# Keys turned later in the step: a move on TensorE and ScalarE in an attention kernel with a routed feed-forward

## The chip, the cores and the metric

The kernel runs on one core of one Trainium2 chip. The metric is the device time of one execution in microseconds (us). The engines are TensorE (PE; its weight loads are listed apart as PEld), VectorE (DVE), ScalarE (ACT), GpSimd (POOL) and SyncE (SP). Matmul results land in PSUM, eight banks of 128 partitions by 512 fp32 words.

## The reference

A block with a residual: layernorm of x (8 batches of 1024 rows, 128 wide), a causal attention that is linear in its scores, and a feed-forward with eight experts of which each row uses two.

```python
q, k, v = heads(Wq), heads(Wk), heads(Wv)            # 16 heads of 64
q = q / max_norm(q); k = k / max_norm(k)             # per batch and head
num = cumsum(v) + einsum(q, cumsum(k outer v))
den = arange(1, n + 1) + einsum(q, cumsum(k))
attn = (num / den) @ Wo.T + bo
probs = softmax(xn @ router_w); top 2, renormalised
expert_out = (silu(xn @ gate[e]) * (xn @ up[e])) @ down[e]
out = x + attn + sum over the two experts of weight * expert_out
```

## The kernel before

The program has an attention phase (up to about 950 us of the profile), a phase that runs tiles of 128 sorted rows through the experts, and a phase that adds the parts. Only the attention phase is touched.

Rows are handled in 64 chunks of 128 (8 batches of 8 chunks). The main loop has a step for each chunk g; c = g % 8 is its place in the batch and b its batch. Each step does several things for different chunks, so that the engines have something to do while they wait for each other. In order, PE issues in a step: `heads_from(g)` (for two groups hg of four head pairs the products with the running sums, L1273 and L1281, then the causal part within the chunk, L1292), `values(g + 2)` (L1157 to L1159 with 512 columns), `project(g - 1)` (output projection, L1329), `outer(g + 1)` (outer products of keys and values, L1307), `keys(g + 2)` (the keys turned, L1241), `scores(g + 2)` (L1255; with c = 0 also `scores(g + 1)`; none with c = 6 and 7), `rank` (with c = 3), `norms` (L1194), `fill` (keys or queries of the next batch, L1157 to L1159 with 256 columns), with an even c also `logits` (8 columns), and `turn(g)` (the finished heads turned, L1318). A step with c = 7 has an order of its own, since the next batch's scale is worked out there, and it is not changed. In the last batch there are no `norms`, `fill` and `logits`.

The small matmuls use part of the array. The profile prints rows*columns of the part: `outer`, `scores` and all of `heads_from` are 64*64, `keys` and `turn` are 64*128, `norms` is 128*32, the rest 128*128.

DVE takes in a step: `heads` (division and copy out, L847 to L856), `x_lo` (with c = 0, 2, 4, 5), `attended` (L880), `state` (adds the outer products to the running sums, L876), `mask` (scores times the causal mask, L839), small routing work (`choose_first`, `choose_second`, `place_rows`) or statistics, `norm_max` (L795), four copies out of `fill` (L785), and with an even c the copy of the logits (L791). With c = 3 `place_rows` lies between `mask` and the copies, with c = 6 `values_parts` (L808 to L815) and `batch_scale`. ACT takes `heads_out(g - 1)` (L591), `values_out` (L585), `keys_out(g + 2)` (L580), `scale_q` (L598), sometimes `normalise` (L561), and four `square` (L574).

PSUM banks are given out by a rule: `psum_order` lists the jobs in the order in which PE does them, job n takes bank n % 8, and before its first matmul PE waits (`wait_bank`) until the job eight places earlier has been read out. The table `FREED` says which semaphore tells that: `e_f` counts the copies of `fill`, `e_L` those of the logits, `e_A` masks, `e_kn` the two halves of `keys_out`, `e_st` states, `e_mx` norm_max, `e_num` heads, `e_nT` heads_out. So the order of the jobs also decides what a matmul waits for. `heads_from` needs four banks, two for each hg; `wait_bank` for the second two is asked just before the second group.

Of the kernel before, what the change touches and what calls it, by code (L numbers as in the profile page):

```python
# [10 lines left out]
C = B * N // P  # L11
# [23 lines left out]
def build(nc, x, wkq, wv, wo, bo, rw, gate_up_w, down_head, down_tail, out):  # L35
# [9 lines left out]
    with ctx:  # L45
# [216 lines left out]
        def psum_order():  # L262
# [22 lines left out]
            for g in range(C):  # L285
                b, c = g // CB, g % CB
                G, more = NCP * (b + 1) + c // 2, b < B - 1
                if c == 0 and g > 0:
                    yield ("O", g - 1)
                yield from uses_N(g)  # L290
                if c == CB - 1 and more:
                    yield from uses_norm(G, 0)
                    yield from uses_fills(G, 1)
                    yield from uses_V(g + 2)
                    yield from uses_norm(G, 1)
                    yield ("O", g - 1)
                    yield from uses_T(g)
                    yield ("C", b + 1)
                    yield from uses_D(g + 1)
                    yield from uses_KT(g + 2)  # L300
                    yield from uses_S(g + 1)
                    continue
                if c in (0, 2, 4) and more:
                    yield from uses_x(G)
                if g + 2 < C:
                    yield from uses_V(g + 2)
                if c == 5 and more:
                    yield from uses_x(G + 1)
                if c == 6 and more:
                    yield ("VC", b + 1)  # L310
                if c > 0:
                    yield ("O", g - 1)
                if g + 1 < C:
                    yield from uses_D(g + 1)
                if g + 2 < C:
                    yield from uses_KT(g + 2)
                if c == 0:
                    yield from uses_S(g + 1)
                if c < CB - 2:
                    yield from uses_S(g + 2)  # L320
                if c == rank_at(b):
                    yield ("R", b)
                if more:
                    if c > 0:
                        yield from uses_norm(G - 1 + c % 2, 1 - c % 2)
                    yield from uses_fills(G, c % 2)
                    if c % 2 == 0:
                        yield from uses_logits(G)
                yield from uses_T(g)
            yield ("O", C - 1)  # L330

# [216 lines left out]
        def _(act):  # L548
# [97 lines left out]
            for g in range(C):  # L646
# [24 lines left out]
                if c == rank_at(b):  # L671
                    act.wait_ge(s_mm, b + 1)
                    act.activation(mm[:], mm[:], ACT.Exp).then_inc(s_exp, 1)
                if g + 2 < C:
                    keys_out(g + 2)
                if c + 3 < CB:
                    scale_q(b, c + 3)
                if c == 5 and b < B - 2:
# [7 lines left out]
                if more:  # L686
                    for f in range(4):
                        square(G, 4 * (c % 2) + f)
                if b == B - 1 and c >= 6:
                    if c == 6:  # L690
                        act.wait_ge(f_w, 16)
                        act.wait_ge(a_N, 2 * (g - 1) + 2)
                        act.wait_ge(f_te, 1)
                    for e in range(4 * (c - 6), 4 * (c - 6) + 4):
                        act.activation(guh[:, e], gu[:, e], ACT.Copy).then_inc(f_wh, 1)
# [454 lines left out]
        def _(pe):  # L1150
# [206 lines left out]
            for g in range(C):  # L1357
# [27 lines left out]
                    project(g - 1)  # L1385
                if g + 1 < C:
                    outer(g + 1)
                if g + 2 < C:
                    keys(g + 2)
                if c == 0:  # L1390
                    scores(g + 1)
                if c < CB - 2:
# [3 lines left out]
                if more:  # L1396
# [3 lines left out]
                        fill(G, 4 * (c % 2) + f)  # L1400
                    if c % 2 == 0:
                        logits(G)
                turn(g)
            project(C - 1)
            pe.wait_ge(e_y, C)
# [97 lines left out]
```

## Time and profile before

| | us |
|---|---|
| median of 3 runs | 1316.72 |
| lowest and highest run | 1312.32 to 1317.18 |
| the profiled execution's own time | 1315.11 |
| its span in the trace | 1313.3 |
| PE busy | 1194.2 (91%) |
| DVE busy | 940.2 (72%) |
| ACT busy | 707.7 (54%) |

The span is what the trace covers; the execution's own time is 1.8 us more. A busy PE is the time in which a matmul was in flight, and two that overlap are counted once, so a run of small matmuls looks as dense as a run of large ones. In the timeline each row is a merged run of instructions of one line: its start, its length up to the end of the last, the line, the operation, the names, the part of the array, the shape and the count. The length overlaps the next row by the time that the last matmul takes to end; what a run costs the engine is read from its start to the start of the row behind it. A bracket gives idle time before the row and what ended it; "issue" is time in which the engine waited for nothing that the profile shows.

### The profile page before, as it was taken

To read this page: it belongs to the slowest core of one execution; us is meant where nothing else is said; L and a number is where in the kernel's file an instruction comes from. 1 tells how busy PE (TensorE), PEld (TensorE's weight loads), DVE (VectorE), ACT (ScalarE), POOL (GpSimd) and SP (SyncE) were. 2 spreads that over 40 slices of the span, in tenths; PEclk is the share of its full clock that TensorE was granted. 3 is DMA by queue.
4 is the path that set the end of the run, shared out by engine and by line. 5 is a ranking of instruction groups with operands and counts; after the bars stand their busy time and mean duration, and the time that the engine had idled before them with its cause. 6 is when DMAs were issued, how large, how long until landed. Compare 5 with 4: busy or idle time off the path is not lost.

```text
span 1313.3 us, 60282 instructions
## 1 busy us (share of the span) xinstructions
PE 1194.2 (91%) x24400; PEld 1053.6 (80%) x24401; DVE 940.2 (72%) x2662; ACT 707.7 (54%) x1683; POOL 366.5 (28%) x599
## 2 busy tenths in 40 slices
PE   6789999999999999999899999998869999999950
PEld 5478878878887887888788788877869999999950
DVE  6778778877877877787788778778845555555534
ACT  4466566647656664665666466555524444444420
POOL 5100111111211111121112111112735555555546
PEclk9999999999999999999999999999979999999985
DMA  6000000000000000000000000020122222222228
GB/s 216 3 4 6 11 12 12 16 11 12 16 12 11 12 17 11 12 14 14 11 12 14 13 12 14 14 99 19 43 84 62 61 61 63 63 61 61 63 84 332
DMA packets 36136, 54.66 MB, mean 42 GB/s; under 512 B 7504, under 2 KB 26608, under 8 KB 35664
## 3 DMA queue, kind: packets, MB, share of 16 engines
q1 hardware_dynamic: 25744, 29.02, 7.2%
q0 software_dynamic: 9024, 18.20, 4.1%
q8 instruction: 179, 2.93, 1.0%
q10 hardware_dynamic: 1152, 4.19, 0.8%
q14 instruction: 37, 0.30, 0.1%
HBM read 28.33 MB, written 23.06 MB: 39 GB/s over the span
## 4 chain that ended last, share of the span: by engine, by line
PE 77%; DVE 14%; issue 4%; DMA 2%; ACT 1%; POOL 1%; SPq 0%; POOLq 0%; DVEq 0%; ACTq 0%
PE bank L1157 10%; PE bank L1159 9%; PE bank L1158 9%; PE bank L1329 8%; PE bank L1436 7%; PE bank L1307 5%; PE bank L1255 5%; PE bank L1292 4%; PE bank L1281 4%; PE bank L1194 4%; PE bank L1429 3%; PE bank L1241 3%; DVE qs L785 2%; PE bank L1318 2%; PE bank L1273 2%
## 5 line engine op out<-in xcount | busy, mean ns | idle before, releaser
L478 POOL COPY xn<-meta 128x2 f32<-128x2 f32 x128 | 26.4, 206 | 712.3 <-PE bank L1292 711.0
L535 POOL DMA_INDIRECT expert_rows<-yt,wdi x136 | 132.6, 975 | 142.4 <-ACT yt L707 116.0
L1157 PE MATMUL bank<-xTh,Wh 128*128 128x256 f32 x512 | 153.0, 299 | 5.0 <-DVEq L812 2.5
L580 ACT ACTIVATE kn<-bank 128x512 f32<-128x512 f32 x128 | 69.5, 595 | 151.9 <-PE bank L1241 151.9
L598 ACT ACTIVATE qs<-qs,cvec 128x128 f32<-128x128 f32 x480 | 146.0, 394 | 0.2 <-DVE cvec L831 0.2
L1158 PE MATMUL bank<-xTh,Wl 128*128 128x256 f32 x512 | 146.0, 285 | 0.0
L1159 PE MATMUL bank<-xTl,Wh 128*128 128x256 f32 x512 | 145.8, 285 | 0.0
L1157 PEld LDWEIGHTS bank<-xTh,Wh 128*128 128x128 f32 x512 | 98.9, 193 | 53.1 <-issue 46.6
L1329 PEld LDWEIGHTS bank<-WoT,numT 128*128 128x128 f32 x1024 | 123.4, 194 | 17.4 <-issue 12.6
L482 POOL DMA_INDIRECT sorted_tokens<-xn,slot x128 | 125.7, 982 | 39.1 <-POOL xn L478 39.1
L1113 DVE TENSOR_TENSOR xtTl<-bank,xtTh 128x128 fp32r<-128x128 f32 x137 | 40.0, 292 | 128.9 <-ACT xtTh L702 119.8
L1329 PE MATMUL bank<-WoT,numT 128*128 128x128 f32 x1024 | 129.1, 280 | 2.1 <-ACT numT L591 1.3
L1436 PE MATMUL bank<-dn,aT 128*128 x828 | 119.5, 281 | 0.0
L707 ACT ACTIVATE yt<-bank,wd 128x128 f32<-128x128 f32 x138 | 50.7, 368 | 122.7 <-PE bank L1436 122.7
L1157 PE MATMUL bank<-guh,xtTh 128*128 x272 | 111.7, 410 | 3.2 <-DVE xtTl L1113 1.6
L856 DVE TENSOR_TENSOR num<-bank,rden 64x256 f32<-64x256 f32 x256 | 108.0, 422 | 8.0
L574 ACT ACTIVATE sq<-ks 128x512 f32<-128x512 f32 x128 | 77.3, 630 | 64.6 <-DVE ks L785 57.6
L839 DVE SCALAR_TENSOR_TENSOR A<-bank,causal 128x512 f32<-128x512 f32 x128 | 82.0, 686 | 41.0 <-PE bank L1255 41.0
L585 ACT ACTIVATE vaug<-bank 128x512 f32<-128x512 f32 x128 | 75.4, 597 | 66.0 <-PE bank L1159 61.4
L1436 PEld LDWEIGHTS bank<-dn,aT 128*128 128x128 f32 x828 | 105.1, 192 | 6.9 <-issue 0.4
L574 ACT ACTIVATE sq<-qs 128x512 f32<-128x512 f32 x128 | 77.5, 630 | 53.1 <-DVE qs L785 44.8
L1158 PEld LDWEIGHTS bank<-xTh,Wl 128*128 128x128 f32 x512 | 99.1, 194 | 0.2 <-issue 0.2
(211 smaller groups left out, 2947.6 us busy)
## 6 DMA issues: line engine op xcount, KB each, us to landing
xt<-sorted_tokens SPq DMA_DIRECT2D x137, 66.0 KB
er<-expert_rows SPq DMA_DIRECT2D x16, 512.0 KB, 6.8
xa<-in_x SPq DMA_DIRECT2D x8, 512.0 KB, 11.2
out<-ot ACTq DMA_DIRECT2D x8, 512.0 KB, 6.9
gu<-in_gate_up_w SPq DMA_DIRECT2D x1, 2816.0 KB, 10.3
expert_rows<-yt,wdi POOLq DMA_INDIRECT x136
sorted_tokens<-xn,slot POOLq DMA_INDIRECT x128, 2.3
wraw<-in_wkq SPq DMA_DIRECT2D x2, 512.0 KB, 5.7
```

The costliest lines, as they stand in the source:

```text
L482: pool.indirect_dma_start(xs_d, bass.IndirectOffsetOnAxis(ap=slot[:, g % XR, k:k + 1], axis=0), xn[:, g % XR, :], None).then_inc(c_out[k][ ...
L535: pool.indirect_dma_start(ys_d, bass.IndirectOffsetOnAxis(ap=wdi[:, r:r + 1], axis=0), yt[:, r, :], None).then_inc(f_sc[r], 16)
L574: act.activation(sq[:, f % 4], src[:, G % NCP, 2 * (f % 4):2 * (f % 4) + 2, :].rearrange("p h i -> p (h i)"), ACT.Square).then_inc(e_sq, 1)
L585: act.activation(vaug[:, g % 2, par, :, 0:DH], pbank("V", g, par)[:].rearrange("p (h e) -> p h e", e=DH), ACT.Copy).then_inc(e_v, 1)
L598: last = act.activation(q_, q_, ACT.Copy, scale=cvec[:, p:p + 1])
L839: dve.scalar_tensor_tensor(A[:, g % 2, par], pbank("S", g, par)[:].rearrange("p (h i) -> p h i", i=DH), 1.0, causal[:].unsqueeze(1).broadc ...
L856: last = dve.tensor_tensor(num[halves(t), 4 * hg:4 * hg + 4, 1, :], v[halves(1 - t), :, 0:DH], rden[halves(1 - t), hg, 1].unsqueeze(2).bro ...
L1157: pe.matmul(dst, ah, bh, start=start, stop=False)
L1158: pe.matmul(dst, al, bh, start=False, stop=False)
L1159: return pe.matmul(dst, ah, bl, start=False, stop=stop)
L1329: last = pe.matmul(pbank("O", g)[:, 0:D], numT[:, p, :], WoT[:, p, :], start=(p == 0), stop=(p == HP - 1))
L1436: last = pe.matmul(bank[6 + s][:, 0:D], aT[:, s, t, :], dn[:, t, bass.ds(ex, 1), :].rearrange("p a f -> p (a f)"), start=(t == 0), stop=(t ...
```

## The change

`keys(g + 2)` moves from behind `outer(g + 1)` to a place directly ahead of `turn(g)`, in every step that has it except c = 7, and `keys_out(g + 2)` on ACT moves from behind `values_out` to a place behind the squares. `psum_order` follows, and so do the banks. No instruction is added or removed, and the order on DVE, POOL and SP is as before.

```diff
@@ psum_order
                 if g + 1 < C:
                     yield from uses_D(g + 1)
-                if g + 2 < C:
-                    yield from uses_KT(g + 2)
                 if c == 0:
                     yield from uses_S(g + 1)
...
                     if c % 2 == 0:
                         yield from uses_logits(G)
+                if g + 2 < C:
+                    yield from uses_KT(g + 2)
                 yield from uses_T(g)
@@ block.scalar
-                if g + 2 < C:
-                    keys_out(g + 2)
                 if c + 3 < CB:
                     scale_q(b, c + 3)
...
                     for f in range(4):
                         square(G, 4 * (c % 2) + f)
+                if g + 2 < C:
+                    keys_out(g + 2)
@@ block.tensor
                 if g + 1 < C:
                     outer(g + 1)
-                if g + 2 < C:
-                    keys(g + 2)
                 if c == 0:
                     scores(g + 1)
...
                     if c % 2 == 0:
                         logits(G)
+                if g + 2 < C:
+                    keys(g + 2)
                 turn(g)
```

On PE, in the middle of a step (here c = 2 of the first batch), from the projection to the first fill, before:

```order
L1329 MATMUL bank<-WoT,numT 128x128 x8
L1307 MATMUL bank<-vaug,kn 64x65 x32
L1241 MATMUL bank<-ident,ks 128x64 x16
L1255 MATMUL bank<-qs,ks 64x64 x32
L1227 MATMUL bank<-rowsum,before 128x8
L1228 MATMUL bank<-rowsum,ones 128x8
```

and after the change:

```order
L1329 MATMUL bank<-WoT,numT 128x128 x8
L1307 MATMUL bank<-vaug,kn 64x65 x32
L1255 MATMUL bank<-qs,ks 64x64 x32
L1227 MATMUL bank<-rowsum,before 128x8
L1228 MATMUL bank<-rowsum,ones 128x8
```

The turned keys (L1241) have left the place between the outer products (L1307) and the scores (L1255).

On PE, at the end of a step with c = 6 (the first batch), from the end of the logits to the second group of the next `heads_from`, with the semaphores that a row waits for, before:

```order
L1159 MATMUL bank<-rwl,xTh 128x8
L1318 MATMUL bank<-ident,num 128x64 [waits e_num,e_n1,e_kn]
L1318 MATMUL bank<-ident,num 128x64 x15
L1273 MATMUL bank<-VC,sel 64x260 [waits e_vc,e_st,e_f,e_mx]
L1273 MATMUL bank<-VC,sel 64x260 x3
L1281 MATMUL bank<-st,qs 64x65 x16
L1273 MATMUL bank<-VC,sel 64x260 [waits e_st,e_f]
L1273 MATMUL bank<-VC,sel 64x260 x3
L1281 MATMUL bank<-st,qs 64x65 x16
```

and after the change:

```order
L1159 MATMUL bank<-rwl,xTh 128x8
L1241 MATMUL bank<-ident,ks 128x64 [waits e_f,e_st]
L1241 MATMUL bank<-ident,ks 128x64 x15
L1318 MATMUL bank<-ident,num 128x64 [waits e_num,e_n1,e_f,e_mx]
L1318 MATMUL bank<-ident,num 128x64 x15
L1273 MATMUL bank<-VC,sel 64x260 [waits e_vc,e_st,e_f]
L1273 MATMUL bank<-VC,sel 64x260 x3
L1281 MATMUL bank<-st,qs 64x65 x16
L1273 MATMUL bank<-VC,sel 64x260 [waits e_st,e_L,e_f]
L1273 MATMUL bank<-VC,sel 64x260 x3
L1281 MATMUL bank<-st,qs 64x65 x16
```

The turned keys stand ahead of `turn` (L1318). The turned heads now wait for a fill's copy and `norm_max` (`e_f`, `e_mx`) instead of `keys_out` (`e_kn`), and the second group (the second L1273) waits for the copy of the logits (`e_L`) as well, which is the last of DVE's copies in the step.

On ACT, from `values_out` of the step with c = 1 of the first batch to that of the next step, before:

```order
L585 ACTIVATE vaug<-bank 128x8x64 x2
L580 ACTIVATE kn<-bank 128x512 x2
L598 ACTIVATE qs<-qs,cvec 128x128 x8
L561 ACTIVATE xn<-xa,nmr,rstd 128x128 x2
L574 ACTIVATE sq<-qs 128x512 x4
L591 ACTIVATE numT<-bank 128x8x64 x2
L566 ACTIVATE xTh<-bank 128x256
L585 ACTIVATE vaug<-bank 128x8x64 x2
```

and after the change:

```order
L585 ACTIVATE vaug<-bank 128x8x64 x2
L598 ACTIVATE qs<-qs,cvec 128x128 x8
L561 ACTIVATE xn<-xa,nmr,rstd 128x128 x2
L574 ACTIVATE sq<-qs 128x512 x4
L580 ACTIVATE kn<-bank 128x512 x2
L591 ACTIVATE numT<-bank 128x8x64 x2
L566 ACTIVATE xTh<-bank 128x256
L585 ACTIVATE vaug<-bank 128x8x64 x2
```

`keys_out` (L580) stands behind the squares (L574) and directly ahead of `heads_out` (L591).

How the places eight earlier in the order of the jobs change, for the waits that the prediction speaks of (hg 0 and hg 1 are the two groups of `heads_from`; fills of a step are numbered 1 to 4):

| wait at the end of step | before | after |
|---|---|---|
| c = 1, 3, 5: hg 0 | no fill, at the latest norms | fills 1 and 2 |
| c = 1, 3, 5: hg 1 | fills 1 and 2 | fills 3 and 4 |
| c = 0, 2, 4: hg 0 | norms or scores, and fill 1 | fills 2 and 3 |
| c = 0, 2, 4: hg 1 | fills 2 and 3 | fill 4 and the logits |
| c = 6: hg 0 | norms and fill 1 | fills 2 and 3 |
| c = 6: hg 1 | fills 2 and 3 | fill 4 and the logits |
| last batch, c = 0: hg 0 | both halves of `keys_out` | the two masks of the first scores |
| last batch, c = 0: hg 1 | the two masks of the first scores | the two masks of the second scores |

## Rows read from the trace of the kernel before

**Rows 1.** Busy time, 120 to 840 us: PE, PEld, DVE, ACT, POOL, clock.
```profile
120.00:840.00 720.00, 694.77 (x17368) 597.94 (x17368) 568.60 (x1593) 439.53 (x984) 114.37 (x198) 1.00 0.04 13
```

**Rows 2.** Waits of PE between 120 and 850 us: total us, times, longest.
```profile
PE bank L1255 <- issue: 4.9, 5, 1.5
...
PE bank L1273 <- DVE ks L785: 2.9, 8, 0.4
PE bank L1273 <- DVE qs L785: 2.3, 6, 0.4
```

**Rows 3.** PE, a step with c = 1: start us, length us, line.
```profile
435.48 1.17 PE L1307 MATMUL bank<-vaug,kn 64*64 64x65 f32 x64
436.57 0.71 PE L1241 MATMUL bank<-ident,ks 64*128 64x64 f32 x16
437.21 1.16 PE L1255 MATMUL bank<-qs,ks 64*64 64x64 f32 x64
438.31 1.07 PE L1194 MATMUL bank<-sq,nsel 128*32 128x512 f32 x8
...
442.36 0.71 PE L1318 MATMUL bank<-ident,num 64*128 64x64 f32 x16
443.00 0.30 PE L1273 MATMUL bank<-VC,sel 64*64 64x260 bf16 x4
443.14 0.64 PE L1281 MATMUL bank<-st,qs 64*64 64x65 f32 x32
443.61 0.28 PE L1273 MATMUL bank<-VC,sel 64*64 64x260 bf16 x4
```

**Rows 4.** Timeline of PE in a step with c = 0.
```profile
307.99 2.10 PE L1255 MATMUL bank<-qs,ks 64*64 64x64 f32 x128
310.01 0.39 PE L1157 MATMUL bank<-xTh,Wh 128*128 128x256 f32 x1
```

**Rows 5.** Timeline of DVE in the step of rows 3.
```profile
440.63 2.53 DVE L785 COPY qs<-bank 128x512 f32<-128x512 f32 x4
```

**Rows 6.** Timeline of DVE in a step with c = 3.
```profile
464.24 1.57 DVE L876 TENSOR_TENSOR st<-bank,st 128x260 f32<-128x260 f32 x4 [0.36 <-PE bank L1307]
466.44 1.29 DVE L839 SCALAR_TENSOR_TENSOR A<-bank,causal 128x512 f32<-128x512 f32 x2 [0.63 <-PE bank L1255]
...
470.94 2.48 DVE L785 COPY qs<-bank 128x512 f32<-128x512 f32 x4
```

**Rows 7.** Timeline of PE where that step ends.
```profile
472.32 0.30 PE L1273 MATMUL bank<-VC,sel 64*64 64x260 bf16 x4 [0.40 <-DVE qs L785]
```

**Rows 8.** Timeline of DVE in a step with c = 6.
```profile
512.24 2.48 DVE L785 COPY ks<-bank 128x512 f32<-128x512 f32 x4
514.62 0.17 DVE L791 COPY L<-bank 128x16 f32<-128x16 f32 x1
```

**Rows 9.** Timeline of PE where that step ends.
```profile
514.21 0.30 PE L1273 MATMUL bank<-VC,sel 64*64 64x260 bf16 x4 [0.42 <-DVE ks L785]
```

**Rows 10.** Timeline of DVE in the step of rows 4.
```profile
309.22 2.48 DVE L839 SCALAR_TENSOR_TENSOR A<-bank,causal 128x512 f32<-128x512 f32 x4 [0.63 <-PE bank L1255]
...
315.65 0.16 DVE L791 COPY L<-bank 128x16 f32<-128x16 f32 x1
```

**Rows 11.** Timeline of PE where that step ends.
```profile
315.24 0.31 PE L1273 MATMUL bank<-VC,sel 64*64 64x260 bf16 x4 [0.17 <-DVE ks L785]
```

**Rows 12.** Timeline of DVE in the last batch, step with c = 0.
```profile
890.04 2.49 DVE L839 SCALAR_TENSOR_TENSOR A<-bank,causal 128x512 f32<-128x512 f32 x4
```

**Rows 13.** Timeline of PE where that step ends.
```profile
891.43 0.30 PE L1273 MATMUL bank<-VC,sel 64*64 64x260 bf16 x4 [1.77 <-DVE A L839]
```

**Rows 14.** Timeline of ACT in the step of rows 3.
```profile
441.41 2.42 ACT L574 ACTIVATE sq<-qs 128x512 f32<-128x512 f32 x4
443.73 1.06 ACT L591 ACTIVATE numT<-bank 128x512 f32<-128x512 f32 x2
```

**Rows 15.** Timeline of PE in the step that follows rows 3.
```profile
446.88 1.39 PE L1329 MATMUL bank<-WoT,numT 128*128 128x128 f32 x11
```

## The prediction

> **What bounds the kernel now.** I read first the table of busy time by stretch. Between 120 and 840 us PE is busy for 694.77 of 720 us (96%), DVE for 568.60 (79%), ACT for 439.53 (61%), with the clock at its upper level all along (1.00) [rows 1]. So in the seven batches that look alike PE sets the pace, and its idle time is small. Then I read who ended it: on the second group of `heads_from` (L1273) PE waited 14 times for a copy of DVE (8 and 6 times, 5.2 us in all, never over 0.4 us), and five times in the scores for "issue", up to 1.5 us [rows 2]. That matters here: DVE is not the bottleneck, but at two places of each batch it is already the last to come. The third view is the timeline of PE, which gives the price of a run of small matmuls from start to start; the fourth is DVE's, at the places where it is late.
>
> **What the move saves on PE.** In a step with c = 1 the outer products take 436.57 - 435.48 = 1.09 us, the turned keys 437.21 - 436.57 = 0.64, the scores 438.31 - 437.21 = 1.10, the turned heads 443.00 - 442.36 = 0.64 [rows 3]. Where 128 scores follow one another they take 310.01 - 307.99 = 2.02 us, so that a second 64 on the same part of the array (64*64) costs 0.92 and not 1.10 [rows 4]. The difference of 0.17 to 0.18 is what a run pays for its two ends. Outer products next to scores are such a run of 128: 2.02 us instead of 1.09 + 1.10, a saving of 0.17. The matmuls have the same part of the array, the same count and nearly the same width (65 and 64 columns). That kinds may differ shows in `heads_from`: its 32 matmuls of L1281, with another line on either side but all on 64*64, take 443.61 - 443.14 = 0.47 us [rows 3], against 0.46 for half of the second 64.
>
> No row shows two runs on 64*128 next to one another. The saving of keys next to turned heads lies between nothing and the 0.18 of the other run; it could be below nothing only if the two disturbed each other, for which I see no reason, as they use different banks. I take 0.15. The Trainium skill (TensorEngine Tiling (Array Packing), Key Properties) says that a change of the tiling mode drains the engine and a change of tile within a mode does not; by it this seam is free, as 0.15 says, and no run here shows it yet.
>
> So a step gains 0.17 + 0.15 = 0.32 us if nothing else is late. There are 62 steps that turn keys, 7 of them with c = 7, so 55 are changed: in each of the seven like batches c = 0 to 6, in the last c = 0 to 5. All of it at 0.32 would be 17.6 us. That is not what comes out, because of the banks.
>
> **What the move makes late.** Everything between the outer products and the end of the logits comes 2.83 - 2.02 = 0.81 us earlier on PE, measured from the step's start, and `heads_from` of the next step 0.32 us earlier. DVE can't follow by 0.81: its masks wait for the scores, but stand behind `state`, which ends at 464.24 + 1.57 = 465.81, while the mask began at 466.44 [rows 6]. So DVE's masks and all behind them come 0.63 us earlier. At the same time the second group of `heads_from` no longer waits for the second or third copy, but for the last one (and with an even c for the copy of the logits). Whether this costs depends on c:
>
> c = 1, 2, 4, 5. In the step with c = 1 the fourth copy ends at 440.63 + 2.53 = 443.16 [rows 5]; 0.63 earlier that is 442.53, ahead even of the first group, which would start at 443.00 - 0.32 = 442.68 [rows 3]. With c = 2, 4 and 5 DVE ends its copies as early or earlier against PE. Nothing is late; 28 steps gain 0.32: -9.0 us.
>
> c = 3. `place_rows` pushes the four copies back: they begin at 470.94 and take 2.48, 0.62 each. The second ends at 472.18, and the second group of `heads_from` starts at 472.32, 0.14 later, after a wait of 0.40 [rows 6, 7]. After the change the copies begin at 470.31, the fourth ends at 472.79, and the group starts at 472.93: 0.61 us later than before instead of 0.32 earlier. Seven times: +4.3 us.
>
> c = 6. There are no scores in this step, and `values_parts` and `batch_scale` fix DVE's time from the outer products on, which do not move. The copies of the fills run from 512.24 for 2.48 us, the third ends at 514.10, the group starts at 514.21; the copy of the logits ends at 514.62 + 0.17 = 514.79 [rows 8, 9]. The group now waits for it and starts at 514.91: 0.70 later. Behind it hangs the chain of the batch's end (heads, copies, squares, norms, scale), all of which moves with it. Six times, and 0.4 in batch 6, where `batch_scale` is absent: +4.6 us.
>
> c = 0. Four masks and the bias lie ahead of the copies. The group starts at 315.24 and waited for the third copy; the copy of the logits ends at 315.65 + 0.16 = 315.81 [rows 10, 11]. The masks begin 0.6 earlier, as the scores now take the place of the keys, so it ends at 315.19 and the group starts at 315.30: +0.06, seven times +0.4 us. In the batches in which the scores stall (below) DVE has caught up, and a part of 0.32 may be had.
>
> The last batch. With c = 0 the four masks begin at 890.04 and end 0.62 us apart; the group waits for the second and starts at 891.43 [rows 12, 13]. It now waits for the fourth, which ends at 892.53: +1.25 us, once. The other five changed steps could gain 1.6 us, but each holds a wait for "issue" that ends at its own time; I count half, -0.8.
>
> ACT hides `keys_out` at nothing: the squares end at 441.41 + 2.42 = 443.83, and `heads_out` takes 1.06 [rows 14], `keys_out`, which has the same two copies of 512 columns, about as much. With the squares 0.63 earlier, `keys_out` and `heads_out` behind them end at about 445.3, and `project` needs that at 446.88 - 0.32 = 446.56 [rows 14, 15]: 1.2 us to spare, about half of that with c = 0. If this cover were gone every step would pay. `keys_out` no longer stands ahead of `scale_q`, which can then start while PE still multiplies; that gains nothing, as the scores waited for it only once. Nothing changes in the queues of SP and POOL.
>
> The sum: -9.0 + 4.3 + 4.6 + 0.4 + 1.25 - 0.8 = +0.75 us. The profiled execution took 1315.1 us, 1.8 more than its span, and 1.6 less than the median of the runs, 1316.7. The sum is 1315.9 on the one and 1317.5 on the other. I predict 1316.5.
>
> **Rivals.** *The late copies don't bite* (faster). If the waits at c = 0, 3 and 6 kept their size, all 55 steps would gain 0.32: 17.6 us off the median of 1316.7, 1299. For it: these are 22 of the 55 steps, so an error of mine there weighs much. Against it: the waits exist already, and the table of the banks says that they now name a later copy. Halfway to the forecast it is 1308.
>
> *The saving is not there* (slower). What a run pays at its ends might belong to the change of operands and not of the part of the array. Then the 9.0 and 0.8 fall away and the costs stay: 9.8 above the forecast, 1326. For it: rows 4 join scores to scores, and the outer products have other operands on both sides. Against it: the 32 matmuls of rows 3, whose neighbours are of another kind and which pay nothing at their ends.
>
> *The instructions come too late* (slower). Five times PE waited for "issue" in the scores, up to 1.5 us and 4.9 in all [rows 2]; the long ones were in steps with c = 0, in the middle of a run of 128, the longest dense run of the program. Now every step with c = 1 to 5 has such a run. It decides if a run of 128 is already long enough. At one in five of 35 steps and 1.5 us that is 10.5 above the forecast, 1327. Against it: the two groups of `heads_from` are as dense and as long, and waited so in few steps. The Trainium skill (Runtime: NRT & Kernel Launch, Instruction fetch mechanics) says that instructions are fetched in sequence, in blocks, ahead of their use, and that this is mostly hidden; by it this rival is nothing and the time stays with the sum. The trace does not quite agree: the 1.5 us of rows 2 are not hidden.
>
> **Chances.** The forecast 0.62; late copies don't bite, wholly or in good part, 0.14; the saving is not there 0.07; the instructions 0.12; ACT's spare time used up, or something I do not see, 0.05. What a measurement of this kernel can tell from no change is about 0.5%, 6.6 us, so "no change" is 1310 to 1323. The forecast's own range is 1311 to 1321: the seam of 0 to 0.18 in 28 steps gives +4.2 and -0.8, the runs' own spread some 2.5 to each side. For 8 in 10 I reach to the middle of the rivals: 1305 to 1326. Faster 0.16 (the first rival, and a little of the forecast), no change 0.65, slower 0.19.
>
> **What would show it.** In the profile after, L1307 and L1255 with c = 1 together from start to start 2.0 us (2.2 would say that nothing is saved), L1241 and L1318 together 1.13 (1.28 likewise). PE's waits on L1273 for DVE's copies grow from 5.2 us to about 18, in steps with c = 0, 3 and 6 alone; if they stay at 5 the first rival holds. A step with c = 3 becomes longer by 0.6 us, one with c = 1 shorter by 0.3. If waits for "issue" in L1255 grow to 10 us or more the third rival holds. If `project` waits for `numT`, I have misjudged ACT. The forecast is wrong if the time lies outside 1310 to 1323.

## The result

The changed kernel took 1323.24 us (median of 6 runs, 1319.95 to 1326.72) against 1315.03 of the kernel before (6 runs, 1312.32 to 1317.18): ratio 1.0064, interval 1.0043 to 1.0085, so 8.4 us slower (5.7 to 11.2). The forecast was no change, 1316.5, and wrong by its own words outside 1310 to 1323. The profiled execution took 1320.09 us, with a span of 1318.3.

### The profile page after: what moved, and what is told of

The parts are those of the page before. It is cut to its first block, busy times and chain, and to the rows that moved or that the text cites. A ratio compares the mean times of both kernels' runs of the same rounds, so it can differ in the third digit from the quotient of the medians.

```text
span 1318.3 us, 60282 instructions
## 1 busy us (share of the span) xinstructions
PE 1188.5 (90%) x24400; PEld 1054.3 (80%) x24401; DVE 935.5 (71%) x2662; ACT 703.6 (53%) x1683; POOL 364.6 (28%) x599
## 4 chain that ended last, share of the span: by engine, by line
PE 73%; DVE 18%; issue 5%; DMA 2%; ACT 1%; POOL 1%; SPq 0%; POOLq 0%; DVEq 0%; ACTq 0%
PE bank L1157 9%; PE bank L1158 8%; PE bank L1159 8%; PE bank L1329 8%; PE bank L1436 7%; PE bank L1307 5%; PE bank L1292 5%; PE bank L1281 4%; PE bank L1255 4%; PE bank L1429 3%; PE bank L1194 3%; DVE qs L785 3%; PE bank L1241 2%; PE bank L1273 2%; DVE ks L785 2%
## 5 line engine op out<-in xcount | busy, mean ns | idle before, releaser
L574 ACT ACTIVATE sq<-ks 128x512 f32<-128x512 f32 x128 | 77.2, 630 | 159.7 <-DVE ks L785 152.8
L1329 PEld LDWEIGHTS bank<-WoT,numT 128*128 128x128 f32 x1024 | 123.4, 194 | 17.1 <-issue 12.3
L574 ACT ACTIVATE sq<-qs 128x512 f32<-128x512 f32 x128 | 77.8, 630 | 109.4 <-DVE qs L785 100.1
L847 DVE RECIPROCAL rden<-bank 128x4 f32<-128x4 f32 x256 | 32.2, 167 | 95.2 <-PE bank L1292 93.2
L1159 PEld LDWEIGHTS bank<-xTl,Wh 128*128 128x128 f32 x512 | 99.7, 195 | 0.0
## 6 DMA issues: line engine op xcount, KB each, us to landing
gu<-in_gate_up_w SPq DMA_DIRECT2D x1, 2816.0 KB, 10.5
```

The lines of the kernel that those rows point to most:

```text
L574: act.activation(sq[:, f % 4], src[:, G % NCP, 2 * (f % 4):2 * (f % 4) + 2, :].rearrange("p h i -> p (h i)"), ACT.Square).then_inc(e_sq, 1)
L1159: return pe.matmul(dst, ah, bl, start=False, stop=stop)
L1329: last = pe.matmul(pbank("O", g)[:, 0:D], numT[:, p, :], WoT[:, p, :], start=(p == 0), stop=(p == HP - 1))
```

## The profile after, beside the rows of before

Busy time between 120 and 840 us (columns as in [rows 1]): PE was busy for 694.77 us of this stretch, now for 683.87. The clock is the same, so 11 us more of PE's time are idle, although not one instruction is new.

```profile
120.00:840.00 720.00, 683.87 (x17284) 592.59 (x17276) 562.43 (x1586) 433.96 (x979) 114.12 (x198) 1.00 0.04 13
```

Who ended PE's waits between 120 and 850 us (total, times, longest), to be held against [rows 2]:

```profile
PE bank L1255 <- issue: 7.5, 11, 1.6
PE bank L1273 <- DVE qs L785: 6.1, 14, 0.5
PE bank L1292 <- issue: 5.7, 7, 1.2
PE bank L1318 <- DVE mx L795: 5.0, 6, 0.8
PE bank L1273 <- DVE ks L785: 4.0, 9, 0.5
```

The waits for copies on L1273 grew from 5.2 to 10.1 us, where I had written about 18. A wait of the turned heads for `norm_max` is new (5.0 us, at c = 6) and takes up time that the group behind it would have waited for the copies; together they are 15.1. The line that I had no term for is L1292. The same view of before has these two:

```profile
PE bank L1241 <- issue: 4.0, 6, 0.8
...
PE bank L1292 <- issue: 1.7, 2, 0.9
```

The 4.0 us on L1241 are six waits of the turned keys at c = 0 for a bank (the profile calls them "issue", but each ends just behind `x_lo`, whose semaphore `e_xs` the keys wait for). With the keys gone the scores have them, so L1241 and L1255 together went from 8.9 (11 times) to 7.5 (11 times). On L1292, the second half of `heads_from`, it is 1.7 us, 2 times, before and 5.7 us, 7 times, after.

PE in the step with c = 1, as in [rows 3]:

```profile
438.98 1.16 PE L1307 MATMUL bank<-vaug,kn 64*64 64x65 f32 x64
439.97 1.11 PE L1255 MATMUL bank<-qs,ks 64*64 64x64 f32 x64
441.01 1.07 PE L1194 MATMUL bank<-sq,nsel 128*32 128x512 f32 x8
...
445.06 0.71 PE L1241 MATMUL bank<-ident,ks 64*128 64x64 f32 x16
445.61 0.67 PE L1318 MATMUL bank<-ident,num 64*128 64x64 f32 x16
446.20 0.31 PE L1273 MATMUL bank<-VC,sel 64*64 64x260 bf16 x4
```

From start to start: outer products and scores 441.01 - 438.98 = 2.03 us (2.0 forecast), turned keys and heads 446.20 - 445.06 = 1.14 (1.13 forecast). Before they were 2.19 and 1.28, so the savings are 0.16 and 0.14: 0.30 us per step, where I had 0.32.

DVE at the end of the step with c = 3 (timeline), to be held against [rows 6]:

```profile
474.43 2.47 DVE L785 COPY qs<-bank 128x512 f32<-128x512 f32 x4
```

And PE there, against [rows 7]:

```profile
475.81 0.31 PE L1273 MATMUL bank<-VC,sel 64*64 64x260 bf16 x4 [0.48 <-DVE qs L785]
...
477.01 0.31 PE L1273 MATMUL bank<-VC,sel 64*64 64x260 bf16 x4 [0.43 <-DVE qs L785]
```

The second group now starts behind the fourth copy (474.43 + 2.47 = 476.90, start 477.01), and the first group waits as well, for the second copy. Then the step with c = 6, DVE's last copy against [rows 8]:

```profile
519.45 0.16 DVE L791 COPY L<-bank 128x16 f32<-128x16 f32 x1
```

And PE, against [rows 9]:

```profile
517.84 0.72 PE L1318 MATMUL bank<-ident,num 64*128 64x64 f32 x16 [0.84 <-DVE mx L795]
519.04 0.30 PE L1273 MATMUL bank<-VC,sel 64*64 64x260 bf16 x4 [0.48 <-DVE ks L785]
...
519.72 0.31 PE L1273 MATMUL bank<-VC,sel 64*64 64x260 bf16 x4
```

The second group comes behind the copy of the logits (519.45 + 0.16 = 519.61), as forecast. Both waits ahead of it, for `norm_max` and for the third copy, are new, but they hold up nothing more: the first group starts 1.2 us later against its step, and 0.5 of that comes back, as the second group waits only for its own copy. In one batch they did cost more. There the granted clock fell to 0.50 from 285.9 to 289.2 us, behind the same two waits (0.84 and 0.48 us), and the 64 matmuls of L1292 took 1.96 us instead of 1.13; that step is 1.4 us longer than its like in the other batches. No term of mine has this, and the profile of the kernel before has no such stretch between 80 and 950 us.

The last batch at c = 0, DVE's masks against [rows 12]:

```profile
894.90 2.48 DVE L839 SCALAR_TENSOR_TENSOR A<-bank,causal 128x512 f32<-128x512 f32 x4
```

PE there, against [rows 13]:

```profile
896.29 0.30 PE L1273 MATMUL bank<-VC,sel 64*64 64x260 bf16 x4 [3.04 <-DVE A L839]
896.40 0.76 PE L1281 MATMUL bank<-st,qs 64*64 64x65 f32 x32
897.49 0.43 PE L1273 MATMUL bank<-VC,sel 64*64 64x260 bf16 x4 [0.33 <-DVE A L839]
897.68 1.11 PE L1281 MATMUL bank<-st,qs 64*64 64x65 f32 x32
898.54 1.90 PE L1292 MATMUL bank<-vaug,A 64*64 64x65 f32 x64
900.38 0.50 PE L1157 MATMUL bank<-Wvh,xTh 128*128 128x512 f32 x1
```

The second group stands 2.59 us behind the start of the masks, where it stood 1.39 behind: 1.20 later, 1.25 forecast. But the first group waits too, and PE is idle for 3.04 us in one piece. The table by stretch (columns as before, the granted clock third from the end) shows what follows, here of after:

```profile
896.20:900.00 3.80, 3.38 (x128) 3.25 (x132) 2.53 (x5) 0.00 (x0) 0.18 (x1) 0.58 0.02 4
```

And of before, behind its own wait:

```profile
891.40:895.00 3.60, 3.57 (x110) 3.27 (x111) 3.50 (x8) 0.84 (x2) 1.95 (x3) 1.00 0.02 5
```

The mean granted clock is 0.58 of 2.4 GHz behind the idle time, mostly the lower level of 1.2 GHz, where it was 1.00. From the second group to the values it takes 900.38 - 897.49 = 2.89 us instead of 893.07 - 891.43 = 1.64: 1.25 more, for which I had no term. How much of this the change brings isn't quite sure. With keys late in this step the clock fell here in all four kept profiles (behind waits of 2.3 to 3.0 us); with keys early it fell in five of thirteen (behind 1.7 to 2.0 us), the kernel before not among them.

Part of the delay is given back where the experts begin. PE's first row there, before:

```profile
967.01 0.45 PE L1417 MATMUL bank<-ident,xt 128*128 128x128 f32 x1 [6.45 <-issue]
```

And after:

```profile
973.22 0.45 PE L1417 MATMUL bank<-ident,xt 128*128 128x128 f32 x1 [3.61 <-issue]
```

PE waits there for something that doesn't move fully with it: 2.8 us of the delay vanish. The experts start 6.2 us later, and the execution ends 5.0 later in these two profiles.

## The experiments

Four theories were held against each other. **A**: the saving is real and waits for banks at c = 0, 3, 6 and in the last batch eat it (the forecast's own mechanism). **B**: the saving isn't there. **C**: denser runs of matmuls run out of instructions, which the profile calls "issue" (my third rival). **C2** is C with another run to blame, told below. **D**: the last batch costs more than its term, by the 3 us wait and the clock. Every ratio is to the kernel before, timed on the same chip; two experiments are compared through it. A trace shows one execution, and two traces differ by a few us even in stretches where the kernels are alike, so what a change is worth is taken from the ratios, and where it lies from the traces. Below, "breaks inside runs" are times of over 0.35 us from one matmul to the next of the same shape with "issue" between them, summed from the first `heads_from` to the end of the seventh batch; the kernel before has 13.3 us of them, the changed one 16.8. A function decides in which steps `keys`, `keys_out` and their banks stand late; where it says no they stand as before:

```diff
+        def late(b, c):
+            return b < B - 1 and c in (1, 2, 4, 5)
...
-                if g + 2 < C:
+                if g + 2 < C and not late(b, c):
                     keys(g + 2)
...
+                if g + 2 < C and late(b, c):
+                    keys(g + 2)
                 turn(g)
```

### Late at c = 1, 2, 4, 5 (as above)

> Keys stand late only in the 28 steps with c = 1, 2, 4, 5 of the seven like batches; all else as before. My forecast's own terms: 28 x 0.32 = 9.0 us less than before (ratio 0.993), as no copy is late there. Theory A (the banks' waits at c = 0, 3, 6 and in the last batch eat a saving that is there) says just this, 6 to 9 us less. Theory B (the saving is not there) says no change within 2 us. Theory C (denser runs of matmuls run out of instructions: the breaks for 'issue' eat it) says 0 to 4 us less, with more than 10 us of 'issue' on the scores in the batches' steps.

Ratio 0.9962 (0.9948 to 0.9976): 5.0 us less (3.2 to 6.8), not 9.0. B falls. PE's waits for "issue" (this kernel's L1299 is L1292 of before, L1262 is L1255, L1248 is L1241):

```profile
PE bank L1299 <- issue: 4.7, 6, 0.9
PE bank L1248 <- issue: 4.4, 6, 0.8
PE bank L1262 <- issue: 4.0, 4, 1.4
```

One of them in PE's timeline, at the start of a step with c = 3:

```profile
569.75 0.75 PE L1299 MATMUL bank<-vaug,A 64*64 64x65 f32 x39
571.27 0.62 PE L1299 MATMUL bank<-vaug,A 64*64 64x65 f32 x25 [0.77 <-issue]
571.82 0.51 PE L1164 MATMUL bank<-Wvh,xTh 128*128 128x512 f32 x1
```

A run of 64 that is broken after 39, for nothing that the profile shows. L1292 has 3.0 us more of this than before, the scores none: 9.0 - 3.0 = 6.0, inside the interval. The rest of the shortfall is within the noise. So C is right in kind, but not in the run for which I had weighed it.

### Late at c = 6 alone: `b < B - 1 and c == 6`

> Keys stand late only in the seven steps with c = 6. Theory A: each of them costs 0.70 us by the wait for the copy of the logits behind the fills' copies, 4.6 to 5 us more than before (ratio 1.0035 to 1.004). Theory B and C: the same wait costs this here too, so this run tells only whether the price of c = 6 is really carried to the end or made up behind the batch. If it is made up, no change.

Ratio 1.0041 (1.0028 to 1.0054): 5.4 us more (3.7 to 7.1), 4.6 by the term; the trace up to the last batch is 3.2 us longer, with 5.1 more in the steps with c = 6 and 7 and 1.9 less in the others, which aren't changed.

### Late at c = 3 alone: `b < B - 1 and c == 3`

> Keys stand late only in the seven steps with c = 3. My forecast's term: seven copies waited for at 0.61 us each, +4.3 us. By the trace of the changed kernel, where such a step is 0.43 us longer: +3.0 us. If breaks for 'issue' (theory C) come on top, one or two of some 1 us each more, so up to 6.

Ratio 1.0030 (1.0020 to 1.0041): 3.9 us more (2.6 to 5.4), 4.3 by the term. In the trace such a step is 0.30 to 0.45 us longer in six batches and 0.05 in the seventh, 2.5 in all, so the price of a step may be nearer 0.4 than the term's 0.61.

### Late at c = 0 alone: `b < B - 1 and c == 0`

> Keys stand late only in the seven steps with c = 0 of the first seven batches. My forecast's term: +0.4 us, no change. Theory C: the run of outer products and 128 scores is 192 matmuls without a slower one between, so breaks there grow, 1 to 3 us more.

Ratio 1.0017 (1.0004 to 1.0030): 2.2 us more (0.5 to 3.9), 0.4 forecast. The two lines for the scores again sum to what they were (8.9 us, the waits of L1241 now with them), and L1299 has 2.0 us more than before:

```profile
PE bank L1262 <- issue: 8.9, 9, 1.9
PE bank L1299 <- issue: 3.7, 3, 1.8
```

### Late in the last batch alone: `b == B - 1`

> Keys stand late only in the last batch (six steps). My forecast's terms say +1.25 - 0.8 = +0.45 us, no change. Theory D, from the trace of the changed kernel (a first group of heads_from that waits some 3 us for a mask in the step with c = 0, PE then at a lower clock for that step, and nothing gained in the other five): the last batch is 4 to 4.5 us longer; at the start of the experts a good part of it is given back where the other stages wait for what does not move, so 2 to 4.5 us more in the time.

Ratio 1.0014 (1.0004 to 1.0024): 1.8 us more (0.5 to 3.2), 0.45 forecast, 2 to 4.5 by D: between the two, with D's lower end inside the interval.

### Late in the last batch at c = 0 alone: `b == B - 1 and c == 0`

> Keys stand late only in one step, c = 0 of the last batch. My forecast's term: +1.25 us. Theory D, from the trace of the changed kernel (a wait of 3.0 us for the second mask, with heads_from at a lower clock behind it): that step is 2.5 to 2.7 us longer. How much of it reaches the end: all six late steps together gave +1.8, the other five nothing, so +1.5 to +2.7.

In the trace the step is 2.55 us longer and waits for the mask 2.3 us in one piece. The time has a ratio of 1.0009 (0.9998 to 1.0021): 1.2 us more (0.3 less to 2.8 more). It can't tell 1.25 from 2.6.

### Late in the last batch at c = 1 to 5: `b == B - 1 and c > 0`

> Keys stand late only in the last batch, with c = 1 to 5 (not with c = 0). Theory D, that the 3 us wait with c = 0 and the lower clock behind it are the loss of the last batch: they are gone, so no change or up to 1.5 us less than before (my forecast's term: -0.8). Theory C, that breaks for 'issue' eat the five steps: +1 to +2 us, as where all six are late.

Ratio 0.9995 (0.9985 to 1.0005): 0.7 us less (2.0 less to 0.7 more); the forecast had -0.8, and nothing gained isn't excluded. So D, as far as it is seen, has its place at c = 0, but the parts (+1.2 and -0.7) fall short of the +1.8 of the whole by about what the intervals leave open.

### Late in the first seven batches alone: `b < B - 1`

> Keys stand late in all 49 changed steps of the first seven batches, the last batch as before. My forecast's terms: -9.0 + 4.3 + 4.6 + 0.4 = +0.3 us against before. Theory D says 4 us below the changed kernel, so about +4 where that is +8. If it is as slow as the changed kernel, the last batch is not to blame and the loss is in the seven like batches (breaks for 'issue' that fall at other places, theory C).

Ratio 1.0049 (1.0033 to 1.0064): 6.4 us more (4.3 to 8.4). Most of the loss is here, 6 us above the sum of my terms. L1299 waits 6.3 us, 7 times, for "issue".

### DVE's order alone

What stood ahead of the four copies of `fill` is put behind them in the first seven batches, with the keys as before. The last two instructions of `values_parts` go into a function of their own, `values_rest`, and the first two of `place_rows`, which free a bank, stay ahead. The lines with + stand behind the copies:

```diff
-                if c == 0:
+                if c == 0 and not more:
                     add_bias(b)
...
-                if b < B - 2 and c == 6:
-                    batch_scale(b + 2)
...
+                    if c == 0:
+                        add_bias(b)
+                    if c == rank_at(b):
+                        place_rows(b)
+                    if c == 5 and b < B - 2:
+                        batch_scale(b + 2)
+                    if c == 6:
+                        values_rest(b + 1)
```

> Keys as before; only DVE's order is changed: the bias at c = 0, most of place_rows at c = 3, batch_scale and a part of values_parts at c = 6 stand behind the four copies. By the waits of before (0.4 at c = 3, about 0.6 at c = 6, 0.17 at c = 0, seven times each) 4 to 8 us less than before. The comparison with the run that has both changes gives the worth of the late keys where no copy is late: theory A 10 to 16 us, theory B nothing, theory C 0 to 6 us.

Ratio 0.9907 (0.9887 to 0.9926): 12.2 us less (9.7 to 14.9), more than the waits themselves promised. In the trace PE no longer waits for a copy of `fill` at all. Up to the last batch it is 11.3 us shorter: 4.7 in the step behind c = 3 (0.6 each), 3.5 with c = 6 and 7, 3.2 with c = 0 and 1.

### DVE's order and late keys together

> Keys stand late in all changed steps of the first seven batches, the last batch as before, and on DVE what stood ahead of the four copies (the bias at c = 0, most of place_rows at c = 3, batch_scale and a part of values_parts at c = 6) stands behind them. Theory A: with the late copies brought forward the whole saving shows, 49 x 0.32 = 15.7 us less than before, and a few more where the waits of before go too: 12 to 20 us less (ratio 0.985 to 0.991). Theory C (the breaks for 'issue' eat it): 5 us less at most, about what the DVE order alone gives. Theory B: as the kernel with the DVE order alone.

Ratio 0.9867 (0.9846 to 0.9888): 17.5 us less (14.8 to 20.3), 1299.70 us, the lowest ratio of this study. No copy is waited for, and the late keys are still worth only 5 us, where A wants 10 to 16. Steps without a break are 0.30 shorter with c = 1 to 5 than under DVE's order alone, but only 0.14 with c = 0 and 6: at c = 6 there are no scores to stand next to, and at c = 0 a wait for a bank still lies between the outer products and them. That makes 12.5 us and not 15.7. Breaks inside runs are 17.1 us against 13.0, which takes 4.1 of it; up to the last batch the trace is 7.4 shorter. L1313 is L1292 of before:

```profile
PE bank L1313 <- issue: 6.3, 9, 1.1
```

The same line under DVE's order alone:

```profile
PE bank L1313 <- issue: 1.9, 2, 1.2
```

### The same, but keys early at c = 0 and 6

> The kernel with late keys and DVE's copies brought forward, but keys early again with c = 0 and c = 6, the steps that gained least (0.14 us each). Theory C: without the late keys at c = 0 and 6 there are some 2 to 4 us fewer breaks for 'issue' than in the kernel with all of them late (17.2 us of breaks inside runs of matmuls), so 0 to 2 us less in time, about 15.5 to 19 less than before. Theory A alone: 2 us more (14 times 0.14 given up).

Ratio 0.9881 (0.9861 to 0.9901): 15.6 us less (13.0 to 18.3), not told apart from the one with all late. Breaks inside runs did not fall (17.1 us; L1313 has 6.2, 8 times), so the steps with c = 1 to 5 bring them.

### The same as DVE's order with late keys, but outer products and scores apart

```diff
-                if c > 0:
+                if c > 0 and not more:
                     project(g - 1)
                 if g + 1 < C:
                     outer(g + 1)
+                if c > 0 and more:
+                    project(g - 1)
```

> The kernel with late keys and DVE's copies brought forward, with project standing between the outer products and the scores (c = 1 to 6 of the first seven batches) instead of ahead of both: keys are still next to the turned heads, but no run of outer products and scores longer than 64 stands there with c > 0. The seam of 0.17 is lost 35 times, 6 us. Theory C, that the unbroken run of 128 is what runs out of instructions: breaks inside runs fall from 17.2 to about 12 to 13 us (what the kernels with early keys show), so in all the time is within 2 us of that kernel. If the breaks stay at 16 to 20 us, the run of 128 is not their cause, and the time is 5 to 8 us longer than of that kernel.

Ratio 0.9959 (0.9945 to 0.9973): 5.4 us less than before, some 12 more than the kernel it was made from, where I had 0 or 5 to 8. The breaks mostly stayed: 15.4 us inside runs, 5.2 us in 8 times on the second half of `heads_from`. So the unbroken run of outer products and scores, the one that my rival had named, is not their cause. The price is of another kind:

```profile
428.51 1.16 PE L1330 MATMUL bank<-vaug,kn 64*64 64x65 f32 x64
429.60 2.05 PE L1352 MATMUL bank<-WoT,numT 128*128 128x128 f32 x16
431.58 1.16 PE L1278 MATMUL bank<-qs,ks 64*64 64x64 f32 x64
432.68 1.07 PE L1217 MATMUL bank<-sq,nsel 128*32 128x512 f32 x8
```

From start to start 1.09 + 1.98 + 1.10 = 4.17 us, against 1.88 for the projection and 2.03 for the pair in the changed kernel, 3.91. With the values ahead of them a step with c = 1 is 0.36 us longer, and it has two more seams between parts of the array. That is what the Trainium skill (TensorEngine Tiling (Array Packing), Key Properties) says of changes of the mode, and the trace agrees on both sides: two seams more cost 0.36 us a step (11.1 us up to the last batch, which is the whole loss), and the seam of keys and turned heads was worth 0.14 (1.14 us instead of 1.28).

### The same, but keys directly behind the scores

Outer products and scores are one run here again (`project` back ahead of them), and `keys_out` stands where it did before.

```diff
                 if c < CB - 2:
                     scores(g + 2)
+                if g + 2 < C and late(b, c):
+                    keys(g + 2)
...
-                if g + 2 < C and late(b, c):
-                    keys(g + 2)
                 turn(g)
```

> The kernel with late keys and DVE's copies brought forward, with the keys directly behind the scores instead of ahead of the turned heads (all changed steps of the first seven batches; their copies on ACT where they stood before). Outer products and scores are still one run on 64*64, but keys, turned heads and heads_from are no longer one run of small matmuls. Theory C2, that this second run (keys, turned heads, heads_from: 168 matmuls that follow one another) brings the added breaks: they fall from 17 us inside runs to about 12 to 13, where the kernels with early keys are; the seam of 0.15 is lost 49 times (7 us), so the time is 1 to 4 us above that kernel, some 13 to 16 below before. If the breaks stay at 16 or more, that run isn't their cause either, and the time is 7 us above that kernel, 10 below before.

Ratio 0.9912 (0.9897 to 0.9927): 11.6 us less (9.6 to 13.6). That is 6 above the kernel it was made from, where I had 1 to 4 if the breaks fell and 7 if they stayed. The intervals of the two leave both open (the traces up to the last batch differ by 3.8), so here the time decides nothing and the trace has to. In it the steps are 0.14 longer, as the lost seam wants, the breaks inside runs fell to 14.0 us (13.3 and 13.0 in the two kernels with early keys), and on the second half of `heads_from` (L1311 here) they went back to where early keys have them:

```profile
PE bank L1311 <- issue: 2.9, 3, 1.1
```

PE's timeline at one place (before and in the step with c = 2 of the fourth batch), with the keys ahead of the turned heads:

```profile
433.54 0.71 PE L1262 MATMUL bank<-ident,ks 64*128 64x64 f32 x16
434.08 0.67 PE L1339 MATMUL bank<-ident,num 64*128 64x64 f32 x16
...
435.86 0.75 PE L1313 MATMUL bank<-vaug,A 64*64 64x65 f32 x37
437.10 0.68 PE L1313 MATMUL bank<-vaug,A 64*64 64x65 f32 x27 [0.49 <-issue]
```

And with the keys behind the scores:

```profile
434.49 0.71 PE L1337 MATMUL bank<-ident,num 64*128 64x64 f32 x16
...
436.31 1.10 PE L1311 MATMUL bank<-vaug,A 64*64 64x65 f32 x64
437.34 0.44 PE L1184 MATMUL bank<-ident,xn 128*128 128x128 f32 x2
```

This is the run that brings the breaks to `heads_from`: keys, turned heads and `heads_from`, 168 matmuls without a slower one between, where it was 152. One trace would be thin for that, but all seventeen agree. In the seven kernels that have the keys ahead of the turned heads with c = 1, 2, 4, 5 the second half of `heads_from` waits 6 to 9 times for "issue" between 120 and 850 us (4.7 to 9.3 us); in the ten others it is 2 or 3 times (1.7 to 3.7 us), wherever else they differ.

### PE's stream moved by 128 places

128 semaphore increments at the start of PE's program, in the kernel before and in the changed one:

```diff
+            for n in range(128):
+                pe.sem_inc(s_pass, 1)
             pe.wait_ge(s_const, 15)
             transpose_x(0)
```

> The kernel before with 128 semaphore increments at the start of PE's program, which only move each later instruction by 128 places in PE's stream. If breaks for 'issue' fall at fixed places of the stream (theory C), PE's waits for 'issue' stand in other steps than before and the time moves by a few us, either way (up to 5). If they don't, the waits stay in the same steps and the time is that of before, up to some 5 us for the increments themselves if they lie on the path at the start.

> The changed kernel with the same 128 increments at the start of PE's program. Theory C: its breaks for 'issue' stand in other steps and the difference to the kernel before moves by some us (it may come out anywhere from +2 to +12). Theory A and D: +8 us to the kernel before, as the changed kernel, apart from what the increments themselves cost in both.

Ratios 1.0036 (1.0021 to 1.0050) and 1.0127 (1.0108 to 1.0147): 4.7 and 16.7 us more than before. So the same change is worth +8.4 us (5.7 to 11.2) with one position of the stream and about +12 with the other; the intervals of these two overlap. The increments themselves delay the first `heads_from` from 70.5 to 83.0 us; from there to the last one the kernel before is 5.3 us faster than without them and the changed one 3.5 slower, by one trace of each. Not all of that is breaks: in the second trace the granted clock also fell four times between 120 and 850 us (once in the changed kernel, never in the kernel before), three times behind the waits at c = 6 and once behind a break of 2.0 us, and this execution was the slowest of its six (1339.66 against 1334.55 in the median). The waits stand in other steps, and the changed kernel has more of them. In the kernel before with the increments:

```profile
PE bank L1299 <- issue: 3.4, 3, 1.5
```

In the changed kernel with them:

```profile
PE bank L1262 <- issue: 9.9, 11, 1.8
PE bank L1299 <- issue: 9.3, 9, 2.0
```

## Why the prediction was wrong

The parts, in us. The third column is the kernel that has this part alone; the last is the wait for "issue" on the second half of `heads_from` between 120 and 850 us, 1.7 before.

| part | forecast | measured alone | L1292 |
|---|---|---|---|
| c = 1, 2, 4, 5 | -9.0 | -5.0 (3.2 to 6.8 less) | 4.7 |
| c = 3 | +4.3 | +3.9 (2.6 to 5.4) | 1.9 |
| c = 6 | +4.6 | +5.4 (3.7 to 7.1) | 1.8 |
| c = 0 | +0.4 | +2.2 (0.5 to 3.9) | 3.7 |
| last batch | +0.45 | +1.8 (0.5 to 3.2) | - |
| sum | +0.75 | +8.3 | |
| all | | +8.4 | 5.7 |

The parts add up to the whole. With intervals of 1.3 to 1.8 us to each side of every part, a few us between them could still hide in that.

- **The saving** was right in kind and nearly in size with c = 1 to 5: 0.16 for outer products next to scores, 0.14 for keys next to turned heads, 0.30 for my 0.32. With c = 0 and 6 it is 0.14, so the first rival's price of 17.6 us (0.32 for all 55 steps) was too high as well.
- **The late copies** were right in place and price: c = 3 and c = 6 cost 9.3 us together, 8.9 forecast. The agreement of the sum is closer than that of the steps (c = 3 by the trace rather less than its term). The first rival falls.
- **The step that failed** is the one in which I let 28 steps gain 0.32 us because "nothing is late". I looked only at other engines. Of the 9.0 us 4.0 did not come, 3.0 of them as breaks on L1292, and c = 0 lost 1.8 in the same way, 2.0 of breaks (its interval only just leaves out the forecast's 0.4). I did have the cause as a rival, at 10.5 us more and a chance of 0.12, but I put it on the run of outer products and scores, and excused `heads_from` because it "waited so in few steps". The scores' waits did not grow (together with those of the turned keys 8.9 us before, 7.5 after), so the sign I had named for this rival, 10 us on L1255, would have missed it. `heads_from` was the run near its limit, and the change put 16 more matmuls ahead of it.
- **The last batch** at c = 0: the wait was sized right for the second group (1.20 against 1.25); missing were the first group, which had not waited, and the lower clock behind 3 us without work, 1.25 us in the trace. What of it reaches the end is 1.8 us (0.5 to 3.2) for the whole batch against 0.45. The five other steps gave what I had put down, as far as can be told.
- **ACT** hid `keys_out`: no wait of `project` between 120 and 850 us. The second rival (saving not there) fell with the first experiment.

So a mechanism failed and not only a size: -9.0 for 28 steps with nothing late, where the time is -5.0 and the instruction stream is what comes late.

Open: how much of the excess is chance of position. Only two positions were tried, and their times don't tell the two apart. Open too is what the falls of the clock at c = 6 cost on average; the one of the changed kernel's profile cost 1.4 us, in one execution.

## What to carry to other kernels

An engine at 96% busy with small matmuls has a supplier too, its own instruction stream: where the waits already name "issue", find every long run of short instructions, and don't count a saving that makes such a run longer or denser as whole until it is measured (here 5.0 of 9.0 us came with c = 1, 2, 4, 5, and about 5 of 12.5 where no copy was late). When a change brings an engine's work forward, the engines behind it need the same lead: freed first (DVE's order, 12 us), then moved, the change pays (17.5 together). And do not price a wait of 2 or 3 us at its idle time alone; read the granted clock behind it.

## What the runs showed of the hardware

The breaks stand at fixed places of PE's instruction stream. Count in the order of PE's program every matmul with its weight load (two places; four for the fp32 matmuls that the trace shows twice) and each of PE's other instructions (the semaphores above all), from the program's start. Between 80 and 850 us the kernel before has 16 idle times of over 0.35 us that the profile puts down to "issue". Six are the waits for a bank at c = 0. The other ten (9.6 us) stand at places 193 to 196 behind a multiple of 256, and nowhere else. The same holds in all seventeen kernels: 13 times after the change (11.9 us), 14 with late keys at c = 1, 2, 4, 5 (11.1), 17 in the kernel with the lowest ratio (12.5), 11 with keys behind the scores (11.4). 571.27 and 437.10 above are two of them. With the 128 increments, which are half a block, 7 and 15 breaks stand at these places again when the increments are counted, and so in other steps, while the waits for banks stay with c = 0. The second half of `heads_from` has the same places in the kernel before and in the changed one, so what the change adds there is not chance of position.

The page has a queue that moves 16 KB a packet:

```profile
q8 instruction: 179, 2.93, 0.9%
```

Between 80 and 850 us it has one packet for each 256 places: 148 for 148 in the kernel before, 147 for 147 in the changed one. Nine of the ten breaks before end 2.2 to 3.0 us after a packet of this queue began. The Trainium skill (Runtime: NRT & Kernel Launch, Instruction fetch mechanics) says that instructions come in blocks of 256, 16 KiB each, and that fetching them is mostly hidden. The trace agrees on the block; hidden it is not always, as the longest such wait is 2.0 us of idle time.

What decides is mostly how fast the block ahead of such a place is used up, from its first matmul to the last one ahead of the break. Over the seventeen traces, of 296 blocks that lasted under 2.5 us, 151 end in a break of over 0.35 us; of 268 that lasted 2.5 to 3.5 us, 55 do; of 1966 that lasted longer, none. A run of 128 small matmuls with their weight loads is such a block of 256 and takes 2.0 us. So a block at that pace is covered about every second time, and which block that is depends on how many instructions stand anywhere ahead. It was not tested by changing the fetching itself.
